# Two runs of indirect transfers without a pause between the transfers

## The reference, cut to what matters

```python
weights, idx = _gate(x, w_gate)            # the 4 best of 16 experts for each token
combine = (one_hot(idx, E) * weights[..., None]).sum(1)
g = silu(einsum('th,efh->tef', x, w1_e))
u = einsum('th,efh->tef', x, w3_e)
routed = einsum('tef,ehf,te->th', g * u, w2_e, combine)
shared = _swiglu(x, w1_s, w3_s, w2_s)      # two shared experts, for all tokens
x = _layernorm(x + routed + shared)
```

## Time and profile before

| | |
|---|---|
| timed runs | 1416.87, 1419.32, 1419.46 us; median 1419.32 |
| profiled execution | 1423.18 us, its span 1421.3 us |
| TensorE busy | 1218.8 us (86%) |
| VectorE busy | 709.6 us (50%) |
| ScalarE busy | 528.7 us (37%) |
| GpSimd busy | 485.6 us (34%) |
| indirect transfers of the second mixture | 64 scatters, 64 gathers |
| granted TensorE clock, mean | 0.912 |

### The profile page before, as it was taken

One profiled execution on the slowest core, in us unless ns is written; L12 is line 12 of the kernel. 1 busy time (PEld: TensorE's weight loads), 2 busy tenths in 40 slices (PEclk: granted clock), 3 DMA queues, 4 the chain that ended last, 5 costly groups with the idle time before them and its releaser, 6 DMA issues. The chain is left out here.

```text
span 1421.3 us, 22346 instructions
## 1 busy us (share of the span) xinstructions
PE 1218.8 (86%) x6643; PEld 801.9 (56%) x6684; DVE 709.6 (50%) x1924; ACT 528.7 (37%) x995; POOL 485.6 (34%) x924
## 2 busy tenths in 40 slices
PE   7689898999869859999999999995988577999990
PEld 3244444444344458767667676784555445778760
DVE  4666666677165426122222222295776425434755
ACT  1257677777656513132222223332333101222210
POOL 6333333121432320122222222113232376806846
PEclk9589999999989958999999999997998577999995
DMA  3970000000000044201010101124200023656743
GB/s 133 331 275 2 1 0 1 0 0 1 1 1 1 1 155 206 74 27 34 31 38 31 38 31 36 50 87 168 87 1 0 19 96 115 215 156 191 213 124 102
DMA packets 64406, 109.20 MB, mean 77 GB/s; under 512 B 7345, under 2 KB 52658, under 8 KB 61362
## 3 DMA queue, kind: packets, MB, share of 16 engines
q1 hardware_dynamic: 54418, 80.96, 16.4%
q0 software_dynamic: 9888, 27.01, 5.9%
HBM read 65.61 MB, written 42.34 MB: 76 GB/s over the span
## 5 line engine op out<-in xcount | busy, mean ns | idle before, releaser
L1390 ACT ACTIVATE f_work<-f_bank,f_ub 128x128 f32<-128x128 f32 x312 | 84.8, 382 | 241.6 <-DVE f_work L1516 221.9
L494 ACT ACTIVATE att_PT<-att_ST 128x1024 f32<-128x1024 f32 (+1 forms) x192 | 148.1, 808 | 66.3 <-PE att_ST L608 34.8
L527 DVE CUSTOM_DVE_ANT_0 att_junk<-att_RB,att_causal_q 128x128 f32<-128x128 f32 (+3 forms) x256 | 120.9, 487 | 60.2 <-PE att_RB L590 48.2
L590 PE MATMUL att_RB<-att_kT,att_qT 96*128 96x512 bf16 (+3 forms) x384 | 122.0, 358 | 23.2 <-DVE att_mx L527 7.2
L1698 PE MATMUL f_bank<-wd_down,f_work 128*128 x624 | 141.2, 380 | 0.5 <-ACT f_work L1390 0.5
L1678 PE MATMUL f_bank<-wu_up,f_work 128*128 x312 | 140.5, 593 | 0.7 <-DVE f_work L1502 0.7
L1698 PEld LDWEIGHTS f_bank<-wd_down,f_work 128*128 128x128 f32 x624 | 115.7, 191 | 14.6 <-issue 0.7
L1339 POOL DMA_INDIRECT Yd<-f_work,f_inv x39 | 38.5, 988 | 236.5 <-DVE f_work L1516 236.5
L1508 DVE COPY f_work<-f_bank 128x512 f32<-128x512 f32 x78 | 54.0, 692 | 120.3 <-PE f_bank L1678 120.3
L2753 PE MATMUL f_bank<-w_w,f_xT 128*128 x376 | 95.5, 398 | 7.8 <-DVE f_xT L2602 3.7
L590 PEld LDWEIGHTS att_RB<-att_kT,att_qT 96*128 96x128 bf16 x384 | 33.9, 99 | 115.5 <-issue 39.8
(11 more groups left out here) (456 smaller groups left out, 2345.3 us busy)
## 6 DMA issues: line engine op xcount, KB each, us to landing
Xd<-g_zero SPq DMA_DIRECT2D x1, 12032.0 KB, 38.2
f_xin<-Xd SPq DMA_DIRECT2D x47, 256.0 KB
Yd<-f_yo SPq DMA_DIRECT2D x47, 256.0 KB
wu_up<-up_w SPq DMA_DIRECT2D x9, 1024.0 KB, 14.4
wd_down<-down_w SPq DMA_DIRECT2D x9, 1024.0 KB, 18.3
w_w<-w SPq DMA_DIRECT2D x6, 768.0 KB, 10.0
wu_up<-Yd SPq DMA_DIRECT2D x16, 256.0 KB, 6.1
w_w<-w SPq DMA_DIRECT2D x1, 2304.0 KB, 18.0
```

The source lines that it names most:

```text
L494: act.activation(buf[:, :, 0:w], ST[:, 2 * (k % 2):2 * (k % 2) + 2, 0:w], ACT.Exp, scale=float(HD) ** -0.5).then_inc(exp_done, 1)
L527: dve.tensor_tensor_reduce(junk[:, k % RING, 0:w], RB[:, bank, 0:w], G.causal_q[:, 512 - w:512], 1.0, LOWEST, ALU.add, ALU.max, to).then_i ...
L590: pe.matmul(RB[:, bank, 0:w], qT[1 - p][0:MROW, r, t * P:(t + 1) * P], kT[1 - p][0:MROW, 512 * c:512 * c + w], start=True, stop=True).then ...
L1390: last = act.activation(hT[:, m, :], bank[:, TB_ + m // 4, (m % 4) * P:(m % 4 + 1) * P], ACT.Gelu, bias=ub[:, ds(e, 1), m])
```

## The change

The pause is left out in the dispatch of half 0 (`n` is 0 there) and in the gather of half 1. The dispatch of half 1 and the gather of half 0 keep it as it was.

```diff
@@ Route1.scatter
             pool.indirect_dma_start(Xd[:, :], bass.IndirectOffsetOnAxis(self.pos[:, n, r, s:s + 1], 0),
                                     G.x_sb[:, self.W.TH * n + s, :], None).then_inc(self.scattered[n], 16)
-            ch.pause(rest)
+            if n:
+                ch.pause(rest)
@@ moe1_stage, gpsimd
                         pool.indirect_dma_start(ga[:, s, r, :], None, Yd[0:P * R * (n + 1), :],
                                                 bass.IndirectOffsetOnAxis(pos[:, n, r, s:s + 1], 0)).then_inc(gathered[s], 16)
-                        ch.pause(route.rest[:, 0:16] if n else route.rest[:, :])
+                        if n == 0:
+                            ch.pause(route.rest[:, :])
```

## The result

| | before | changed |
|---|---|---|
| median of the timed runs (6 each) | 1421.35 us (1416.87 to 1426.1) | 1436.17 us (1428.86 to 1437.89) |
| ratio, 95% interval | | 1.0104 (1.0083 to 1.0125) |
| profiled execution, its span | 1423.18, 1421.3 us | 1435.12, 1433.2 us |
| first scatter to first transposition of the loop | 64.46 us | 66.35 us |
| first transposition to first issue of the last gather | 180.5 us | 180.3 us |

The changed kernel is 1% slower; 1412.8 us was forecast. The table's stretches sum to +15.2 us; the stages ahead of the first scatter, which the change doesn't touch, were 3.3 us shorter in this execution (1118.92 against 1122.20), and the difference of the spans is the 11.9 us left. Nearly all of it lies in the last gather.

What follows compares the result with a forecast made beforehand. The prediction took TensorE to bound most stages and GpSimd a few, among them the first dispatch and last gather. Its terms, 0.4 + 2.9 + 3.2 = 6.5 us, off the median of 1419.32 gave 1412.8 us, range 1408 to 1420.

Steps and rivals of the forecast that it cites:

- The price of a pause: Between indirect transfers: a pause costs 0.40 - 0.30 = 0.10 us, since most of the gap is the next transfer's start.
- Rival 4: Transfer interval stays at 1.35 us because something the memset hid in paces long rows: 1419.3 us; chance 0.07.
- (a): Three scatters of half 0 at the end of the recurrent stage: 0.4 us saved, bounds 0 and 0.8.
- (b): 29 scatters of half 0 in the mixture stage: 28 shorter intervals save 2.9 us, bounds 0 and 11.2.
- rival 2: Dispatch stall worsens as semaphore increments get through poorly without pauses; product 7.8 us late, about 1423.9 us; chance 0.14.
- Rival 3: Dispatch stall goes away and VectorE's tail is again the bound: 14.7 us saved, 1404.6 us; chance 0.08.
- part (c): Last gather, 32 transfers with GpSimd setting the pace: 3.2 us saved, bounds 0 and 12.
- Rival 1: First dispatch's saving is hidden, VectorE's tail and the load being level: only 3.6 us saved, 1415.7 us; chance 0.19.

Runs made afterwards that it cites:

- e11: The changed kernel again, unaltered, in another group of runs, against the kernel before: 1407.1 us, ratio 0.9966.
- e1: Kernel before without the pauses in the dispatch of half 0 only, last gather keeping its short ones: 1422.12 us, ratio 1.0009.
- e19: Kernel before without the pauses in the dispatch of half 0 only, repeated on another chip: 1423.11 us, ratio 1.0017.
- e3: Kernel before with pauses of 256 columns instead of 16 in the dispatch of half 0: 1412.65 us, ratio 0.9946.
- e12: The kernel before, unaltered, run for its profile beside the unaltered changed kernel: 1413.58 us in its one run.
- e2: Kernel before without the pauses in the last gather only, dispatch as before: 1434.92 us, ratio 1.0098.
- e4: Kernel before with a 16-column memset and no wait for it after each transfer of the last gather: 1434.42 us, ratio 1.009.
- e20: Kernel before without the pauses in the last gather only, repeated on another chip: 1430.68 us, ratio 1.0094.
- e5: Kernel before with the last gather's pauses kept for the first four tiles and removed for the last four: 1408.55 us, ratio 0.9986.
- e8: Kernel before with an always-met wait and no memset in place of each last-gather pause: 1406.64 us, ratio 0.9978.
- e9: Kernel before with a 128-column memset and no wait for it after each last-gather transfer: 1408.23 us, ratio 0.9991.
- e16: Kernel before with a 128-column memset and no wait after each last-gather transfer, repeated on another chip: 1410.46 us, ratio 0.9998.
- e18: Kernel before without last-gather pauses, GpSimd waiting for the last shared sums before the third tile's gathers: 1420.19 us, ratio 1.0049.
- e10: Kernel before with pauses of 128 columns instead of 16 in the dispatch of half 0: 1409.84 us, ratio 1.0006.
- e13: Kernel before with an always-met wait and no memset in the last gather, repeated on another chip: 1408.58 us, ratio 0.9977.

## Why the prediction was wrong

1. **The price of a pause was right.** Transfers without a pause stand 0.30 us apart in rows of 29 and of 32, as in the row of four fetches. Rival 4 is out. Where nothing stalls, the kernel gains 4.7 us (e11), of the 6.5 that were the sum; the interval, 2.5 to 7.1, takes both in, and point 5 has what the profiles say of the rest.

2. **Part (a) was too high.** From the first scatter to the step of the normalisation behind the second it takes 2.48 us against 2.74, 0.26 less, but to the first of the 29 scatters 10.81 against 10.91: 0.1 of its 0.4 us gets there.

3. **Part (b) was right in its size and wrong in what comes through.** The run of 29 scatters takes 35.68 us against 38.60, 2.9 less, and the load follows. "If the release of ScalarE hangs on the end of the scatters, all of it comes through: VectorE's tail behind it is the same work" failed: the tail from the product of step 3 on is the same, 11.82 us, but at the end of the scatters ScalarE and VectorE are a step further back, and that product comes 8.04 us behind the last issue instead of 3.08. That is 5.0 us more, against 3.0 us that the scatters give, (a) and (b) together: the stretch is 1.9 us longer, and the ratios of e1 and e19 show no gain. That is the mechanism of rival 2, with a smaller price: the product comes 1.9 us late, where rival 2 had 7.8. Rival 3 needed the stall to go away, which the change doesn't do on a chip that has it (e1, e19); the longer pause of e3 does.

4. **The step that failed is part (c), by its bound.** It reads "Bounds 0 and 30 x 0.40 = 12", with nothing below 0, and rival 2, which held the right mechanism, let the last gather off: "the same in the last gather could cost only beyond the 2.3 to 3.3 us that VectorE waits per tile". I took the gather for a pair of GpSimd and VectorE, with TensorE out of it, from a stretch, 1400 to 1410 us, in which TensorE has nothing to do. But up to 1389.6 it has: two shared sums stand in VectorE's queue ahead of six tiles, and VectorE works in order. Two sums that start 12 and 21 us behind the end of TensorE's products (1401.65 and 1410.77 against 1389.61) stop all six, and their 6 x 2.73 = 16.4 us can't overlap the transfers any more. The last tile's weighting starts 19.62 us behind the last issue instead of 2.75, +16.9, less the 3.3 us of shorter gathers: the 13.5 us in the table. With VectorE idle 2.3 to 3.3 us per tile, the cover was for a delay of each tile, not for one that holds the queue.

5. **Rival 1 was right in part; the sum took (b) in full.** It was to find VectorE's tail level with the load. Where nothing stalls, the kernel before has 5.32 us to spare there (e12), and the first transposition comes 3.7 us earlier with the change. But in e11 VectorE's tail has become the bound of the first copy. It overlaps the dispatch of half 1, which also starts earlier, and two of its small steps take 1.06 and 1.27 us (lines 2381 and 2388) where e12 has 0.17 for each; that the overlap is the reason isn't shown. So from the first scatter to the first issue of the last gather e11 gains 2.4 us (231.6 against 234.0), though its last scatter is issued 3.35 us earlier.

6. **The stall itself I had read rightly, and from one chip.** I took it for a property of the kernel, with the gap of 3.9 us between profile and median as a small doubt. It goes with the group of runs, and so perhaps with the chip: with the short pause in the dispatch, the stretch to the first transposition takes 62.8 to 65.1 us on the three with the stall (before, e2, e4, e20) and 55.2 to 55.9 on the three without (e5, e8, e9, e12 to e16, e18). The page "SBUF — State Buffer" of the Trainium skill, section "SBUF: two separate sides", says that TensorE and ScalarE never wait on anyone. I had set that against the stall, but the section is about the ports into SBUF. ScalarE's 19.06 us of idle time with its operand in place (changed kernel) are real, and no run here says that a port is their cause, so the trace neither bears the sentence out nor refutes it.

**What is shown and what is not.** Shown: the loss is the last gather's (e1, e2, e19, e20); a longer pause frees the dispatch on a chip with the stall (e3); the sign of the change isn't the same in every group of runs (e11). Read from traces only: that increments come late, and that they are TensorE's. In the changed kernel ScalarE's SiLUs (line 2534) and VectorE's shared sums (line 2580) wait by the program for TensorE's results, and these had ended long before; VectorE's products (line 2574) wait for ScalarE's too, so their waits don't tell the two apart. TensorE's waits for VectorE stay on time (1384.20 behind a product that ended at 1384.14), and so do the 0.30 us of the transfers. No run took the shared sums out from between the tiles on a chip with the stall, which would have tested their part in the loss. Open: whether the free time or GpSimd's wait lets an increment through, since e8 and e9 never met a stalling chip and e4 took both away at once; where the stall of the dispatch ends between the 0.41 us from one transfer's end to the next one's start, which has it, and e3's 0.61, which doesn't, since e10 didn't meet one; and what sets the two kinds of chip apart.

## What to carry to other kernels

Before a pause between indirect transfers is taken out, look in every engine's queue for instructions that wait for TensorE while the transfers run, and count what stands behind them in order: that, and not the idle time per tile, is what a late start costs. An unexplained idle time ("issue" or "remote") of many microseconds that ends with a run of indirect transfers is a warning, and lengthening the pause is as good a test as removing it. And compare on more than one chip before an edit of this kind is called a gain or a loss. Last, where two engines' work ends level, a saving in one of them comes through only until the other is the bound.

## What the hardware showed that I had not expected

- VectorE can start 12 and 21 us behind the end of the TensorE products that it waits for, while indirect transfers are issued every 1.25 us (line 2580 of the changed kernel).
- The same program takes about 1420 us in three groups of runs and about 1411 us in three others; some 9 us of it are one stall in the dispatch (64.46 against 55.85 us, before and e12), and 2.3 us lie in the loop up to the last gather (180.5 against 178.2 us, before and e13 to e16). Of these, 1.8 us belong to the stall as well: VectorE's first copy comes 3.0 us behind the first transposition instead of 1.2, and e3, without the stall on the same chip as e2, has 1.2 and 178.8 us. The change is worth +1.04% in a group with the stall and -0.34% in one without, each measured once.
- 0.30 us of the distance between two indirect transfers are the next one's own start: a memset of 0.14 us without a wait fits inside and lengthens nothing (e4).
- 0.2 us more between two scatters (1.58 us apart instead of 1.37) removed the dispatch's stall: with 5.6 us more of pauses in it the kernel is 0.54% faster (e3).
